# Attention with its row sums taken over four steps at a time, filler products behind every other pair, and half of Q's second block moved behind attention's first steps

## What is computed

```
q, k, v = layernorm(x) @ wq, @ wk, @ wv        # 2048, 512, 512 columns
q, k = rope(q), rope(k)
attn = softmax(q k^T / 8)                      # over all 4096 keys, no mask
x = x + layernorm((attn v) @ wo)
h = relu(layernorm(x) @ sign(up_weight)^T * up_scale)          # 8192 columns
x = x + layernorm((h @ sign(down_weight)^T * down_scale) * output_scale)
```

## Time and profile before

| | |
|---|---|
| time, median of 3 runs | 2291.59 us (2290.8 to 2291.95) |
| the profiled execution's own time | 2293.13 us |
| its span on the slowest core (core 2) | 2291.6 us |
| spans of cores 0 to 7 | 2281.1, 2287.8, 2291.6, 2279.5, 2289.0, 2281.5, 2282.1, 2287.0 us |
| granted TensorE clock, mean of core 2 | 0.989 |
| PE busy, ACT busy, DVE busy | 2192.3, 1485.8, 944.9 us |
| first and last start of an exponential, core 2 | 248.4 and 1316.9 us |

### The profile page before, as it was taken

One profiled execution on the slowest core, in us unless ns is written; L12 is line 12 of the kernel. 1 busy time (PEld: TensorE's weight loads), 2 busy tenths in 40 slices (PEclk: granted clock), 3 DMA queues, 4 the chain that ended last, 5 costly groups with the idle time before them and its releaser, 6 DMA issues.

```text
span 2291.6 us, 49322 instructions; the slowest of 8 cores (2279.5 to 2291.6 us)
## 1 busy us (share of the span) xinstructions
PE 2192.3 (96%) x19840; PEld 1074.0 (47%) x19840; DVE 944.9 (41%) x1817; ACT 1485.8 (65%) x1443; POOL 58.4 (3%) x99
## 2 busy tenths in 40 slices
PE   4999899999999999999999899999999999999996
PEld 2455455554555544444444344444444444444442
DVE  4888344444444445443453543211221121122168
ACT  5766599999999999999999933222222222222224
POOL 1000100000000000000000000000000000000000
PEclk9999899999999999999999999999999999999998
DMA  8984502230222010025534655533333444444453
GB/s 257 264 287 168 103 22 73 82 91 2 72 72 82 2 20 2 2 49 110 112 81 83 151 195 221 201 147 147 147 147 147 148 158 160 160 160 164 162 213 147
DMA packets 59631, 287.15 MB, mean 125 GB/s; under 512 B 14352, under 2 KB 14352, under 8 KB 35728
## 3 DMA queue, kind: packets, MB, share of 16 engines
q1 hardware_dynamic: 47520, 246.70, 29.6%
q0 software_dynamic: 10704, 36.87, 9.5%
q10 hardware_dynamic: 1184, 0.43, 0.1%
HBM read 290.29 MB, written 29.36 MB: 139 GB/s over the span
## 4 chain that ended last, share of the span: by engine, by line
PE 87%; DVE 4%; ACT 4%; issue 3%; DMA 2%; DVEq 0%; ACTq 0%; POOL 0%; SPq 0%
PE woP L62 38%; PE sc L62 12%; PE pv L543 12%; PE pv L552 7%; PE fP L696 6%; PE fP L62 6%; PE kvP L62 3%; PE qP L62 2%; ACT ex L526 2%; PE tpP L66 1%; DMA xb<-x 1%; DVE dacc L1192 1%; DMA W<-wkv 1%; PE fP L66 1%; DMA wstg<-wkv 1%
## 5 line engine op out<-in xcount | busy, mean ns | idle before, releaser
L526 ACT ACTIVATE ex<-sc,ebias 128x1024 bf16<-128x1024 f32 x1024 | 1043.1, 1126 | 36.4 <-PE sc L62 30.6
L979 ACT ACTIVATE pan<-stg 128x2048 bf16<-128x2048 f32 x128 | 234.6, 1898 | 597.6 <-PE woP L62 578.8
L62 PE MATMUL sc<-QT,KT 64*128 64x256 bf16 x4096 | 329.1, 274 | 24.8 <-ACT ex L526 23.1
L543 PE MATMUL pv<-ex,VT 128*64 128x256 bf16 x4096 | 324.6, 280 | 2.6 <-DVE nsA L564 1.0
L62 PEld LDWEIGHTS sc<-QT,KT 64*128 64x128 bf16 x4096 | 155.3, 95 | 200.3 <-issue 185.0
L543 PEld LDWEIGHTS pv<-ex,VT 128*64 128x64 bf16 x4096 | 185.5, 110 | 113.3 <-issue 112.9
L62 PE MATMUL woP<-xn2Ta,pan 128*128 128x512 bf16 x1024 | 231.0, 379 | 1.1 <-DVE xn2Tb L1067 1.1
L62 PE MATMUL woP<-xn2Tb,pan 128*128 128x512 bf16 x1024 | 231.0, 379 | 1.1 <-DVE xn2Tb L1067 1.1
L62 PE MATMUL woP<-pan,hidb 128*128 128x512 bf16 x1024 | 223.5, 379 | 0.0
L62 PE MATMUL woP<-pan,hida 128*128 128x512 bf16 x1024 | 223.5, 379 | 0.0
L552 PE MATMUL pv<-ex,VT 128*32 128x256 bf16 x4096 | 207.2, 279 | 0.0
(11 more groups left out here) (108 smaller groups left out, 1696.8 us busy)
## 6 DMA issues: line engine op xcount, KB each, us to landing
stg<-upw SPq DMA_DIRECT2D x64, 1024.0 KB, 7.7
stg<-dnw SPq DMA_DIRECT2D x64, 1024.0 KB, 7.4
xb<-x SPq DMA_DIRECT2D x32, 1024.0 KB, 11.6
xnT_rl<-xsp SPq DMA_DIRECT2D x48, 512.0 KB, 3.4
wo<-wo POOLq DMA_DIRECT2D x48, 512.0 KB, 7.3
xsp<-xnT_rg SPq DMA_DIRECT2D x24, 512.0 KB, 6.5
out<-dacc SPq DMA_DIRECT2D x16, 512.0 KB, 2.7
wstg<-wkv SPq DMA_DIRECT2D x4, 1024.0 KB, 18.9
```

The source lines that it names most:

```text
L62: return self.do("tensor", lambda e: e.matmul(out, lhsT, rhs, start=start, stop=stop), "t" if sig else None)
L526: t_e[s] = p.s(lambda e: e.activation(ex[s % NE][:], sc[s % 3][:], AF.Exp, bias=ebias[:], scale=0.125))
L543: p.do("tensor", lambda e, s=s, o=o, r=r, c=c, k2=k2: e.matmul(pv[64 * r:64 * r + 64, 0:256], VT[:, o:o + 64], ex[s % NE][:, r * 512 + c * ...
L979: t_sign[n, k] = p.s(lambda e: e.activation(pan[n % 2][:, k * 2048:(k + 1) * 2048], stg[sl][:], AF.Sign))
```

## The change

1. `s_pv(g)` now issues only the products with V. The sums of steps g to g+3 are issued together by a new `s_sum`, behind every second pair (g % 4 == 2), 16 products in a row. NE rises from 4 to 8, so that `ex` holds long enough.
2. Fillers run once per pair, by `filling(least)`: behind the pairs without sums if there is any credit, behind those with sums only if the credit is at least 4. The rate is 1.27 a step (1.36 in the last quarter); the credit may reach 9 and is cut to 7 when it is spent.
3. `VT` holds V alone; the ones are a tile `ones` of their own, and the second memset of ones at the end of stage 1 is gone. Some buffers move.
4. Stage 1 makes 12 tiles of Q, one in each even iteration from 8 on; the weights of the second block are loaded into `wqA` after tile 10. Tiles 4 to 7 of the second block become fillers (two calls of `q_pair`) between the halves of the first `kv_fill`. The next block's `wqA` is loaded after them.
5. The pause until step 10 ahead of the first filler is gone.

```diff
@@ stage 1 @@
-            if t == 8:
-                load_wq0(1, t_kv[8])
-            if t >= 8 and qi < 16 and t % 3 != 2:
+            if t == 10:
+                p.wait("gpsimd", t_kv[t])
+                for k in range(4):
+                    t_wl["wa"].append(p.dma("gpsimd", wqA[:, k * 2048:(k + 1) * 2048],
+                                            wq[128:256, k * 2048:(k + 1) * 2048], "wa%d" % k))
+            if t >= 8 and t % 2 == 0:
                 q0_mm(qi)
                 q0_rope(qi)
                 qi += 1
...
-        t_ones2 = p.do("gpsimd", lambda e: e.memset(
-            bass.AP(VT, 64 * 192 + 64, [[32 * 768, 128], [192, 64], [1, 64]]), 1.0), "g")
@@ q_fill @@
             load_blk("wb", W2, wkv, 1, [s1] * 4)
-            load_blk("wa", wqA, wq, 2, [s1] * 4)
             p.wait("sync", *s1)
             for r in range(2):
                 reload(r)
-            yield from until(10)
-            yield from kv_fill(0, range(0, 32, 2), 0)
+            yield from kv_fill(0, range(0, 16, 2), 0)
+            for t in (4, 6):
+                yield from q_pair(1, t, "wa", wqA)
+            load_blk("wa", wqA, wq, 2, [(q_last[0],)] * 4)
+            yield from kv_fill(0, range(16, 32, 2), 8)
@@ pacing @@
-        def step():
-
-            credit[0] = min(credit[0] + (1.13 if now[0] < 3 * NS // 4 else 1.25), 4.0)
+        def filling(least):
+
+            if credit[0] < least:
+                return
+            credit[0] = min(credit[0], 7.0)
             while credit[0] > 0:
                 c = next(fill, None)
                 if c is None:
                     break
                 credit[0] -= c
+
+        def step(s, rate):
+            now[0] = s
+            credit[0] = min(credit[0] + rate, 9.0)
...
             s_pv(g)
+            if g % 4 == 2:
+                s_sum(g - 2)
             if g % 16 == 14:
                 s_norm(g + 1)
-            step()
-            now[0] = g + 1
-            step()
+            rate = 1.27 if g < 3 * NS // 4 else 1.36
+            step(g, rate)
+            step(g + 1, rate)
+            filling(1 if g % 4 == 0 else 4)
```

More of the change, by code:

```diff
@@ L157, in build_nc @@
         cs_f = [at(f"cs_f{i}", Z + 158 + 0.375 * i, 96, F32) for i in range(4)]
-        NE = 4
-        ex = [at(f"ex{i}", Z + 192 + 2 * i, 1024, BF16) for i in range(NE)]
+        NE = 8
+        ex = [at(f"ex{i}", Z + (192 if i < 4 else 64) + 2 * i, 1024, BF16) for i in range(NE)]
         nsA = at("nsA", Z + 200, 512, F32)
@@ L417, in q0_flip @@
             t_qt[i // 8, i % 8] = qt_free[0]
[L419 to L425, removed]
+        t_wq0 = [None]
+        t_wl = {"wa": []}
         t_w0 = [None] * 4
@@ L471, in build_nc @@
         k_flip(NT - 1)
-        if qi == 16 and (1, 7) not in t_qt:
-            q0_flip(15)
-        p.wait("gpsimd", p.now("s"), p.now("t"), p.now("xs0"), p.now("xs1"), p.now("xs2"))
-        t_ones2 = p.do("gpsimd", lambda e: e.memset(
-            bass.AP(VT, 64 * 192 + 64, [[32 * 768, 128], [192, 64], [1, 64]]), 1.0), "g")
+        if q_flipped < 12:
+            q0_flip(11)
         stage1 = (p.now("v"), p.now("s"), p.now("t"))
@@ L536, in s_pv @@
                 pp = pi // 4
-                p.wait("tensor", t_e[s], t_ones, t_ones2)
+                p.wait("tensor", t_e[s], t_ones)
                 if k2 == 0:
@@ L546, in s_pv, with s_sum @@
                             start=k2 == 0 and c == 0, stop=k2 == 15 and c == 1, skip_group_check=True))
-            for s in (g, g + 1):
+        def s_sum(g):
+            for s in range(g, g + 4):
                 k2 = steps[s][3]
@@ L602, in build_nc @@
         f_free = [None]
-        t_wl = {}
         def load_blk(buf, dst, src, row, waits):
@@ L735, in kv_fill @@
             kv_last[g] = tk
-            kv_done[g] = True
+            kv_done[g] = 30 in order or g == 1
         kv_last = [None, None]
@@ L926, in ready @@
             pp = pi // 4
-            return pp < 2 or kv_done[pp - 2] and all((pp, t) in t_qt for t in range(4 * hf, 4 * hf + 4))
+            return (hf, pp) in ((0, 0), (0, 1), (1, 0)) or (pp < 2 or kv_done[pp - 2]) and all((pp, t) in t_qt for t in range(4 * hf, 4 * hf + 4))
         fill = fills()
@@ L934, in build_nc @@
         for g in range(0, NS, 2):
-            now[0] = g
+            now[0] = max(now[0], g)
             while not ready(g + 4):
-                now[0] += 1
-                step()
+                step(now[0] + 1, 2.0)
+                filling(0)
             s_mm(g + 3)
```

41 lines of the change are left out of this document (22 added, 19 removed).

## The result

| | before | after |
|---|---|---|
| median of the runs | 2291.77 us | 2318.58 us |
| the profiled execution | 2293.13 us | 2318.94 us |
| span of the slowest core | 2291.6 us (core 2) | 2317.4 us (core 3) |
| spans of cores 0 to 7, mean | 2285.0 us | 2309.7 us |

The ratio is 1.0115 [1.0092 to 1.0138]. The forecast was 2295 us with a range that ended at 2310, so it was too low by 24 us and the time lies outside the range; "slower" was its likeliest sign, at 0.38. In some executions of every kernel the cores of one die, or of both, ran up to 16% longer at a lower granted clock; the ratios leave these out.

The account below looks back on a forecast made before the run. PE was taken to bound stage 1; in attention PE and ACT were both full, ACT setting the pace. Stage 1 -14.2, start +5.8, steady part +13.4 (-8 + 13.4 + 8), `wo` -2.0 gave +3.0: 2295 us, range 2276 to 2310.

Parts of the forecast that it names:

- Stage 1: Stage 1: four Q tiles leave the path, 14.7 us, less 0.5 us for loads; -14.2 us.
- The start: Start of attention: PE waits for the first load of `W2` after five exponentials; +5.8 us on core 2.
- Relief: Attention's steady part: fewer groups of sums and fillers free PE time that ACT had waited for; -8 us, between -17 and 0.
- Bursts: Attention's steady part: rows of six or seven fillers behind 16 sums lose 0.80 us each; +13.4 us.
- Ends of passes: Attention: the next V product waits for DVE's copy of `pv`, some 0.3 us in 53 of 63 passes; +8 us.
- (b): Rival, ends of passes: DVE's copy and its latency become the limit, nothing is relieved; total +19, 2311 us; chance 0.23.
- The first load of `wo`: First output products: five pairs instead of four lie between the load's issue and its use; -2.0 us.
- (c): Rival, start of attention: first load of `W2` lands sooner, start costs +2.6, total -0.2, 2291.4 us; chance 0.10.
- (a): Rival, attention: relief had in full, pass ends cost nothing; steady part -3.6, total -17.0, 2275 us; chance 0.22.
- three signs of being wrong: Profile signs: idle time at the start under 5 us, mean start distance under 1.015, stage 1 ending later than 237.

Follow-up runs that it names:

- s4_alone: The kernel before with sums of four steps and V without ones alone, 16 Q tiles in stage 1, fillers behind every step at 1.18 and 1.30; ratio 1.0006.
- both_fine: The changed kernel with fillers asked for behind every single step, at 1.30 and 1.40, credit at most 4.0, the first held back to step 10; ratio 1.0007.
- pause_rope: The changed kernel with first fillers held back to step 10 and fillers' rope work on DVE held back in the last steps of each pass; ratio 1.0059.
- b_stage1_fast: The kernel before with 12 instead of 16 Q tiles in stage 1, sums behind every pair, fillers at rates of 1.30 and 1.40; ratio 1.0098.

## Why the prediction was wrong, step by step

**Stage 1, -14.2: right as a mean.** -15.0; core by core it is -10.0 to -19.3, so on one core the agreement would have been luck.

**The start, +5.8: right in kind, a little small as a mean.** Five exponentials, 10.85 us of idle time, clock 0.50 behind it, as written. As a mean over the cores it is +8.2. The forecast had 5.8 on core 2 and 9.4 on core 3 and summed with the 5.8; measured are +2.0 on core 2 (39.2 to 41.2 us for steps 0 to 32) and +12.2 on core 3 (32.7 to 44.9). It also held that core 2 stays the slowest; core 3 was (2317.4 against 2304.4 us).

**Relief, -8: this is the step that failed.** It took half of what PE had to spare, and gave the four Q tiles, 14.7 us of PE work put into a stretch where both engines were full, no term of their own: "the planner spends much of it" stood for them. Measured over steps 32 to 1023, the sums of four alone are +0.9 us (s4_alone less before) and the moved tiles +15.1 (both_fine less s4_alone), together +16.0 against -8. A relief exists only once the tiles have filled PE, where the steady part shows at most some 13 us of it, and the tiles cost more. The bound from below was an inconsistency: 17 us is ACT's whole waiting time, and it could not be given back while PE's work there also grew.

**Bursts, +13.4: right in price, and only part of the cause.** The row shown lost 0.77 us as forecast (0.80), and the 19 long rows behind sums in the steady part lost 16.3 together, 0.86 each. But such rows lost 7.4 already before, not 3.8 (2.0 of it at one place, step 751). And the rows of seven behind the other pairs, which "are shorter by 0.55 and fit", do not fit: 43 of them lost 16.7 us. That is why taking all fillers away from behind the sums gave 3.5 us in the steady part, not 13.

**Ends of passes, +8: right in kind, too small at single places.** 45 waits where some 50 were forecast, but 27.3 us of them, 0.6 each instead of 0.3, and up to 1.9. By its own rows the forecast should have had more: 1.09 less the 0.55 of the scores and the 0.12 of a change leaves 0.42 a pass and not 0.3, that is 22 us of PE and not 16. Rival (b) named this mechanism but priced only the copy and its latency. What it left out is the order on DVE: the ropes of a lump of fillers stand ahead of the copy. Holding them back took the waits to 14.7 us and the steady part down by 10.7.

Bursts and ends of passes together were forecast at +21.4; after less both_fine is 17.7 in the steady part and -1.6 in the last quarter, 16.1. So grouping was priced well as a sum, by luck: part of it was put on the wrong rows, and what the other rows lose was missing. The miss of 18.7 us in steps 32 to 1023 (+32.1 against +13.4) is the relief's 24.0 less 5.3.

**The first load of `wo`, -2.0: not seen.** PE waits as long as in the earlier trace rows, in three pieces:

```profile
PE fP L62 <- DMA wo<-wo: 2.2, 3, 1.3
```

**Rivals.** (c) was right on core 2 and fell on the cores that set the time. On core 2 the first load of `W2` landed 6.2 us after its issue (9.5 before), and steps 0 to 32 took 2.0 us more, where (c) had 2.6. On core 3 it was issued at 240.8 and PE went on at 250.07, 9.3 us later, where it had landed after 6.3 before. The spread stayed (6.2 to 9.2 us on the eight cores) and changed cores. The estimate of 4.4 us by the Trainium skill ("DMA: Bandwidth & Descriptors", section "Anatomy of one DMA") is not borne out by this trace. (a) fell, and its sum was wrong: with -3.6 in the steady part the total is -14.0 and not -17.0, so 2278 us and not 2275. (b), at 2311 us, was nearest, through half of its mechanism. The mean distance of exponentials, forecast as 1.03, is 780.2 / 736 = 1.060. None of the three signs of being wrong came, since all three looked for a fault at the start, in stage 1 or on the fast side; none would have shown a slower steady part.

What stays open: which part of the grouping's remaining cost (pause_rope less both_fine, 8.4 us in the steady part) is waits for `kvF`, waits for `nsA` of under 0.6 us, or the length of the rows, and what the sums of four are worth with 12 Q tiles at an equal pace of fillers. No run separates these.

## What to carry to other kernels

Work that is moved from a stage with one full engine into a stage where two are full needs a price of its own there, at its whole length, before any saving is set against it; and a saving of PE time is worth only what PE lacks, here nothing with 16 tiles in stage 1 and some 2 to 11 us with 12. Background work is cheapest in small, even pieces: grouping it saves changes between kinds of products, but it removes the cover from short waits elsewhere (the copy at the end of a pass), and the work that it queues on a second engine in program order gets ahead of that engine's urgent step. When such background work has deadlines, look for the single long stall and the leftover at the end before judging its pace by the steady part.

## What the runs showed of the hardware

The clock did not answer alike to two idle times of the same length. After the wait of 1.74 us that ended at 402.69 the granted clock was 0.50 (1.2 GHz), and eight products with V took 1.06 us; after one of 1.74 us that ended at 438.19 it was 1.00 and they took 0.63. The two stretches, of PE in after, then the second wait and ACT behind it:

```profile
402.70:404.70 2.00, 2.00 (x18) 0.50 0.03 8
438.20:440.20 2.00, 2.00 (x32) 1.00 1.04 209
```

```profile
438.19 0.63 PE L539 MATMUL pv<-ex,VT 128*64 128x256 bf16 x8 [1.74 <-DVE nsA L564]
...
439.80 6.14 ACT L523 ACTIVATE ex<-sc,ebias 128x1024 bf16<-128x1024 f32 x6 [0.87 <-PE sc L62]
```

The same wait of PE cost ACT 0.87 us where the clock held and 1.94 where it fell. No run tests what decides between the two.

The price of a change between kinds of products came back as time of PE, but not all of it as time of the kernel. The forecast read 0.12 us, with 0.213 us for a product; no row shows that figure, and with the 0.216 of the earlier trace rows the six fillers of the earlier trace rows leave 0.11. both_fine has one group of sums fewer than b_stage1_fast in each of the steady part's 184 groups of four steps: 184 x 0.11 = 20 us. The stretch is 13.0 us shorter, and PE's idle time in it, as a mean of the cores, grew from 18.3 to 29.4 us, so PE worked 24.1 us less. Of that 4.5 are fillers by the estimate above, and 19.6 are left for the changes, 0.11 each.
